# Head values multiplied by the output weights beforehand, four feature buffers, and the constant rows moved: a gated attention with mixture of experts on one core

## The reference

```python
# block 1: attention of 16 heads of 64, gated
qkv = x @ w_qkv.T; q, k, v = heads of qkv
gate = sigmoid of the scores of the 32 best tokens of a batch (by a small network on
       the mean of q over heads, layer-normalized), sigmoid(-1e9) for all others
dots = q k^T * 64**-0.5 * (gate_i * gate_j)
x = layernorm(x + (softmax(dots) v) @ w_out.T + b_out)
# block 2: causal attention of 16 heads of 8, then 8 experts of width 256, the best 2 of each token
x = x + mla(rmsnorm(x, g1)); x = x + moe(rmsnorm(x, g2), gate_w, w1, w2)
x = layernorm(...)
```

## Time and profile before

| | us |
|---|---|
| profiled execution, its own time | 694.79 |
| its span, first to last instruction | 692.7 |
| PE busy | 646.5 (93%) |
| DVE busy | 485.0 (70%) |
| ACT busy | 418.9 (60%) |
| POOL busy | 250.3 (36%) |
| mean PE clock granted, share of 2.4 GHz | 0.977 |

### The profile page before, as it was taken

One profiled execution on the slowest core, in us unless ns is written; L12 is line 12 of the kernel. 1 busy time (PEld: TensorE's weight loads), 2 busy tenths in 40 slices (PEclk: granted clock), 3 DMA queues, 4 the chain that ended last, 5 costly groups with the idle time before them and its releaser, 6 DMA issues.

```text
span 692.7 us, 14079 instructions
## 1 busy us (share of the span) xinstructions
PE 646.5 (93%) x5409; PEld 434.2 (63%) x5424; DVE 485.0 (70%) x1045; ACT 418.9 (60%) x764; POOL 250.3 (36%) x319
## 2 busy tenths in 40 slices
PE   7888798889899999999999999999999999999885
PEld 3476554455556667666766676766666667756774
DVE  2745556765687868876887787778777867754765
ACT  3452445666677666766675768575867676673431
POOL 8133101321333343344333533353334443443432
PEclk9999888999999999999999999999999999999998
DMA  8500000000000000000000000000000000000000
GB/s 317 183 18 16 1 1 1 1 2 1 1 1 1 1 1 2 17 1 1 1 18 1 1 2 16 2 1 2 17 1 2 1 16 1 1 16 1 1 16 16
DMA packets 10068, 12.15 MB, mean 18 GB/s; under 512 B 1609, under 2 KB 8210, under 8 KB 9746
## 3 DMA queue, kind: packets, MB, share of 16 engines
q1 hardware_dynamic: 9250, 11.25, 4.9%
q10 hardware_dynamic: 752, 0.01, 0.1%
HBM read 9.16 MB, written 2.10 MB: 16 GB/s over the span
## 4 chain that ended last, share of the span: by engine, by line
PE 70%; DVE 8%; ACT 5%; issue 3%; POOL 1%; POOLq 0%; ACTq 0%; DVEq 0%
PE turn L990 15%; PE turn L983 11%; PE psV L1043 11%; PE psW L1031 9%; PE psS L1016 6%; PE turn L945 5%; PE turn L935 3%; DVE negmax L1232 3%; PE psS L1005 2%; ACT prob L1151 2%; PE turn L953 2%; PE turn L964 1%; DVE late L1292 1%; ACT X L1062 1%; PE turn L884 1%
## 5 line engine op out<-in xcount | busy, mean ns | idle before, releaser
L1151 ACT ACTIVATE prob<-psW 128x1024 f32<-128x1024 f32 (+1 forms) x192 | 182.9, 953 | 108.1 <-PE psW L1031 107.8
L1232 DVE TENSOR_REDUCE negmax<-psS 128x2 f32<-128x1024 f32 (+2 forms) x249 | 198.9, 819 | 31.3 <-PE psS L1016 30.8
L853 POOL TENSOR_SCALAR_AFFINE_SELECT prob<-prob 128x512 f32<-128x512 f32 x128 | 79.8, 635 | 251.6 <-ACT prob L1151 251.6
L1292 DVE SCALAR_TENSOR_TENSOR late<-late,turn 128x512 f32<-128x512 f32 x128 | 87.5, 684 | 66.9 <-ACT late L1121 66.7
L990 PE MATMUL turn<-wexp,late 128*128 128x128 f32 x1024 | 129.3, 280 | 1.8 <-DVE late L1292 1.3
L990 PEld LDWEIGHTS turn<-wexp,late 128*128 128x128 f32 x1024 | 120.6, 193 | 10.1 <-issue 6.0
L1121 ACT ACTIVATE late<-turn 128x512 f32<-128x512 f32 x128 | 76.4, 597 | 63.0 <-PE turn L983 60.0
L861 POOL TENSOR_TENSOR late<-late 128x512 f32<-128x512 f32 x62 | 79.3, 1279 | 72.2 <-DVE late L1311 72.2
L1031 PE MATMUL psW<-qT,kT 26*128 26x256 f32 (+2 forms) x512 | 92.9, 399 | 8.7 <-ACT prob L1151 8.0
L1005 PE MATMUL psS<-kT,qT 24*128 24x256 f32 (+1 forms) x498 | 90.8, 401 | 1.0 <-DVE negmax L1232 0.9
L1031 PEld LDWEIGHTS psW<-qT,kT 26*128 26x128 f32 x512 | 43.1, 183 | 76.7 <-issue 52.6
(11 more groups left out here) (265 smaller groups left out, 894.9 us busy)
## 6 DMA issues: line engine op xcount, KB each, us to landing
prob<-in_xT SPq DMA_DIRECT2D x4, 512.0 KB, 6.4
X<-in_x SPq DMA_DIRECT2D x1, 2048.0 KB, 16.5
out<-late SPq DMA_DIRECT2D x8, 256.0 KB, 2.2
prob<-in_wqkvT SPq DMA_DIRECT2D x1, 1024.0 KB
late<-in_w SPq DMA_DIRECT2D x1, 1024.0 KB, 9.8
prob<-in_wqkvT SPq DMA_DIRECT2D x2, 256.0 KB, 3.7
late<-in_woutT SPq DMA_DIRECT2D x1, 512.0 KB
base_all<-base_rows SPq DMA_DIRECT2D x2, 256.0 KB, 3.2
```

The lines of the kernel that those rows point to most:

```text
L853: pool.affine_select(out=blk, in_=blk, compare_op=ALU.is_ge, fill=0.0, base=0, pattern=[[0, 4], [1, P]], channel_multiplier=-1).then_inc(s ...
L1151: A(into, src, ACT.Exp).then_inc(s["exp_ready"], 1)
L1232: last = V.tensor_reduce(negmax[:, u % 2, c, 2 * p:2 * p + 2], scores_in(b, n)[:, :, HALF * i:HALF * i + P * (c + 1)], AX, ALU.max, negate ...
L1292: V.scalar_tensor_tensor(out=hid[:, e % 2, k, :], in0=tanh[:, n % 2, :], scalar=1.0, in1=bank("hidden", b, n)[:, :], op0=ALU.add, op1=ALU. ...
```

## The change

In stage 1: (a) four feature buffers instead of two, and PE runs two features ahead; ACT takes the square root straight from PSUM with the epsilon as its bias, without DVE's pass. (b) Slot numbers start at 1, so that one DVE pass goes. (c) After the product of value and output weights over all heads, PE makes it for each head apart (`WVO`), and ACT copies it; the chosen tokens are multiplied with `WVO` instead of the value weights (four matmuls of 512 columns), and the heads' weights with that, all 16 added up in one bank; DVE gives the weights out in three parts. The outputs of the heads, their copies and the second product go. (d) The order around the gather: query and key matmuls wait only for the copied tokens; the base row comes after them; slot matmuls earlier; scores in two parts. (e) DVE adds the base rows of batches 0 and 1 in stage 1; POOL adds the other six in stage 2 (`rows`). `base_all` lies in the room of `oT`. In stage 2: (f) for batch 0 ACT takes a square root of variance terms for `xr`, in place of POOL's power; chunk by chunk signals; the first transposed half is handed over early; tables are loaded ahead by small activations. (g) Many places are changed, four of six `half parts` come between the first scores, and there are 32 fillers instead of 27.

```diff
-            A(Fc[:, t % 2, 0:HALF], ...) ; wait for v_done, g_ps at t - 1
+            A(Fc[:, t % 4, :], ...) ; wait for v_done, g_ps at t - 3
-                if t >= 1 and t + 1 < B:
-                    features(t + 1)
+                if t + 2 < B:
+                    features(t + 2)
-                V_.tensor_scalar(var[:, at], var_in[h][:, 0:HALF], LN_EPS, None, ALU.add).then_inc(g_used, 1)
+            for k in range(H):
+                i, rows = head_at(k) // 2, slice(DH * (k // NI), DH * (k // NI) + DH)
+                last = mm(bank[(0, 2, 3, 4)[k // 4]][:, D * (k % 4):D * (k % 4) + D], WvT[rows, i, :], WOUT[rows, i, :],
+                          start=True, stop=True, tile_position=(DH * (k // NI), 0))
...
-            unread(8)
+            for n in range(NH):
+                last = mm(bank[6 + n][:, :], selh[:, n, :], slot[:, :], start=True, stop=True)
...
+            for part, heads in enumerate(WEIGHTED):
+                pe.wait_ge(bdT_ready, part + 1)
+                pe.wait_ge(v_sb, heads.stop // 4)
+                for k in range(heads.start, heads.stop):
+                    last = mm(bank[1][:, 0:D], BDT[:, k, :], VW0[:, k, :], start=(k == 0), stop=(k == H - 1))
             last.then_inc(dl_ps, 1)
...
-            pool.wait_ge(bdT_ready, 1)
-            for b in BY_POOL:
-                ...
+            dve.wait_ge(base_in[0], 16)
+            for b in range(ROWS_EARLY):
+                V_.tensor_tensor(X[:, ts, :], X[:, ts, :], base_all[:, b, :]..., ALU.add)
...
-GATE_AT, SUM_AT, ADD_AT = 1.0, 1.21, 1.32
+GATE_AT, SUM_AT, ADD_AT = 1.0, 1.01, 3.42
-UNITS = {"usual": (13, 1.0, 3), 6: (13, 1.0, 3), 7: (13, 1.0, 4)}
+UNITS = {"usual": (13, 1.0, 3), 6: (13, 1.0, 3), 7: (14.5, 1.0, 4)}
-SELECT_AT = (2.0, 4.8, 5.2, 5.21)
-VALUE_AT = (4.0, 6.5, 6.5, 7.5)
+SELECT_AT = (2.3, 3.5, 4.2, 4.21)
+VALUE_AT = (4.0, 6.5, 7.5, 7.5)
-EARLY = {0: -40.35, 1: -37.2}
-NORMALIZE_EARLY = {0: -26.0, 1: -24.4}
-NORMAL_FROM = {2: 1.7, 3: 13.7, 4: 25.7, 5: 46.7, 6: 67.7, 7: 97.7}
+EARLY = {0: -41.35, 1: -25.1}
+NORMALIZE_EARLY = {0: -8.2, 1: -9.9}
+NORMAL_FROM = {2: -2.3, 3: 13.7, 4: 22.7, 5: 40.7, 6: 67.7, 7: 97.7}
-    ("half parts", 4): -39.85, ("half parts", 5): -39.75,
+    ("half parts", 2): -10.2, ("half parts", 3): -8.2, ("half parts", 4): -6.2, ("half parts", 5): -4.2,
-    UNREAD_AT: 27 places, from -11.2
+    UNREAD_AT: 32 places: -40.12, -40.11, -32.9, -30.0, -25.0, -24.5, -9.2, -7.2, -5.2, -1.2, -0.2, 0.8, 1.8, 2.8, ..., 187.3
+ROWS_FROM, ROWS_PITCH = -11.5, 1.5
...
+                if what == "rows":
+                    pool.wait_ge(keep["base_in"][b // HB], 16)
+                    pool.tensor_tensor(xb, xb, keep["base_all"][:, b, :]..., ALU.add).then_inc(s["rows_ready"], 1)
+                elif what == "first root" and b == 0:
+                    act.wait_ge(s["both_var"], 1)
+                    A(both[:, :], ve1[:, 0, 1, :], ACT.Sqrt).then_inc(s["both_root"], 1)
```

More of the change, by code:

```diff
@@ L172, in _ @@
                              ).then_inc(base_in[n], 16)
-            for n in range(NH):
-                sp.wait_ge(base_in[n], 16)
+            sp.wait_ge(base_in[0], 16)
         @block.gpsimd
@@ L308, in _ @@
             pe.wait_ge(masks, 2)
[L309 removed]
+            pe.wait_ge(std_ready, 1)
             unread(IN_GATE)
@@ L384, in _ @@
             base_rows(1)
-            pe.wait_ge(bdT_ready, 1)
-            pe.wait_ge(v_sb, 2)
-            for k in range(H):
-                h = head_at(k)
-                i = h // 2
-                rows = slice(DH * (h % 2), DH * (h % 2) + DH)
-                last = mm(bank[(6, 4)[i // 4]][rows, P * (i % 4):P * (i % 4) + P], V0[:, DH * h:DH * h + DH],
-                          BDT[:, k, :], start=True, stop=True)
-            last.then_inc(o_ps, 1)
-            pe.wait_ge(o_sb, 2)
-            for i in range(NI):
-                last = mm(bank[6][:, 0:D], OT[:, i, :], WOUT[:, i, :], start=(i == 0), stop=(i == NI - 1))
+            values(2)
+            values(3)
+            for part, heads in enumerate(WEIGHTED):
[3 more added lines that the diff above has]
+                    last = mm(bank[1][:, 0:D], BDT[:, k, :], VW0[:, k, :], start=(k == 0), stop=(k == H - 1))
             last.then_inc(dl_ps, 1)
@@ L442, in _ @@
             A(gv[:, :], scores[:, :], ACT.Sigmoid).then_inc(sig, 1)
+            for k in range(4):
+                act.wait_ge(wvo_ps, k + 2)
+                A(WVO[:, 4 * k:4 * k + 4, :], bank[(0, 2, 3, 4)[k]][:, :].rearrange("p (k d) -> p k d", d=D),
+                  ACT.Copy).then_inc(wvo_sb, 1)
             wqkv, wgate, wexp2, w1all = keep["wqkv"], keep["wgate"], keep["wexp2"], keep["w1raw"]
@@ L1081, in _ @@
                       ACT.Copy).then_inc(is_free("half outputs", 0, n), 1)
+                elif what == "first root" and b == 0:
+                    act.wait_ge(s["both_var"], 1)
+                    A(both[:, :], ve1[:, 0, 1, :], ACT.Sqrt).then_inc(s["both_root"], 1)
+                elif what == "nextT" and b == 0:
+                    A(xrT[:, 0:HALF], src[:, 0:HALF], ACT.Copy).then_inc(s["xrT_first"], 1)
+                    A(xrT[:, HALF:T], src[:, HALF:T], ACT.Copy).then_inc(is_free(what, b, n), 1)
                 elif what == "nextT":
@@ L1189, in _ @@
                 elif what == "offset":
+                    if b == 0:
+                        dve.wait_ge(s["both_root"], 1)
+                        own(V.reciprocal(both[:, :], both[:, :]))
+                        for c in range(C):
+                            V.tensor_scalar(xr[:, c, :], X[:, c, :], mv1[:, 0, c, 0:1], both[:, c:c + 1], ALU.subtract,
+                                            ALU.mult).then_inc(s["xr_first"], 1)
                     dve.wait_ge(s["rs1_ready"], b + 1)
```

279 lines of the change are left out of this document (152 added, 127 removed).

## The result

The changed kernel takes 689.55 us (median of 7 runs, 685.92 to 691.00) against 694.79 for the kernel before, measured beside it (7 runs). The ratio is 0.990, with a 95% interval of 0.9862 to 0.9938. All ratios and counts of runs in this document leave out those that lie over 1.5% above the fastest of their kernel (one of e2_add_early, two of e10_slots_and_fillers), while the medians are of all runs. Faster was right; the size was not: 678.5 was forecast, and 689.55 lies above the range of 672 to 686. The profiled execution took 689.55 us, with a span of 687.1.

A forecast was written before the change was run, and what follows sets the result against it. PE was taken to bound the full batches, and a chain through several engines everything before the first attention weights. Gains 8.1 + 5.6 + 1.5 + 1.5 - 0.4 = 16.3 took 694.8 to 678.5 us; range 672 to 686.

The forecast's parts named there:

- Feature buffers and bias row: Stage 1, 0 to 25 us: last variance 3 us earlier, mostly hidden by the bias-row wait; gain 0.3, bounds 0 to 2.9.
- Rival A: Stage 1: the bias row lands early, so PE doesn't wait for it; 2.6 us more gain, 675.9 us, chance 0.12.
- Rank and gather: Stage 1, ranking to scores: gains of 0.45, 1.35 and 0.65 us; second gather at 47.6 instead of 50.36.
- The product made beforehand: Stage 1: value-output products hidden; PE takes 12.0 us from second gather through heads; stage 2 at 60.2, whole stage gaining 8.1.
- Head of stage 2: Stage 2 start to first attention weights: 32.3 us instead of 37.9; gain 5.6, bounds 3.0 to 8.3.
- Rival B: Head of stage 2: it gives back all it gains; 684.1 us, chance 0.15.
- rival C: Stage 2: POOL's six row additions hold up every VectorE pass beside them, 8.8 us; 687.3 us, chance 0.06.
- First batch: First batch's attention: three added fillers fill idle time or lift the clock; -1.5 us, bounds +1.3 and -4.
- Tail: Last batch's end: first product 1 us later, following sequence closed up; -1.5 us, bounds +1 and -3.
- Rival D: Expert steps: later POOL additions free banks late and stall PE, 19 us over 64 steps; 697.7 us, chance 0.06.
- Rival E: Stage 1: heads wait for the fourth value copy instead of following the softmax parts; under 1 us, no separate chance.

The follow-up runs named there:

- e2_add_early: The changed kernel with POOL's additions of the experts' outputs and the residuals put back at their earlier places; 685.56 us, ratio 0.9855.
- e10_slots_and_fillers: The changed kernel with the eight fillers put back ahead of the four slot matmuls, which stay ahead of the gather; 687.31 us, ratio 0.985.
- e7_two_buffers: e3_slots_late with two feature buffers instead of four and the products of one step issued ahead; 684.89 us, ratio 0.9867.
- e1_bout_first: The changed kernel with the bias row loaded ahead of x instead of behind it; 688.16 us, ratio 0.9888.
- e3_slots_late: The changed kernel with the slot matmuls moved back behind the values and eight full fillers in their place; 683.34 us, ratio 0.9832.
- e11_slots_late_bare: The changed kernel with the four slot matmuls moved behind the values, but without the eight fillers; 689.96 us, ratio 0.9937.
- e14_fewer_fillers: The changed kernel without the three fillers that the change adds in the first batch's attention; 688.85 us, ratio 0.9901.
- e4_old_places: The changed kernel with all step places of stage 2 as before the change, stage 1 and each step's code as changed; 695.30 us, ratio 0.999.
- e5_select_early: e3_slots_late with the two places of e2_add_early, and POOL's first select of each group at 2.0 instead of 2.3; 680.62 us, ratio 0.98.
- e12_after_again: The changed kernel itself measured once more, with no difference; 690.47 us, ratio 0.9932.
- e9_all: e5_select_early with the bias row loaded ahead of x; 676.23 us, ratio 0.9739.

## Why the prediction was right or wrong

**Feature buffers and bias row: right, the exact time by luck.** The transposes at 20.34 (near 20.3 forecast) and the scores at 23.95 (near 24) answer to the first two signs that it named. The last variance came at 17.50, not near 16.6, since ScalarE's steps are 1.1 us apart and not 0.9; the wait for the bias row hides that. In the other profiles with the bias row behind x the transposes start between 20.3 and 22.2, so the 0.3 us of gain is smaller than what one execution differs from another. e7_two_buffers shows that the buffers bring nothing there that can be measured, and e1_bout_first that the wait was for the bias row. Rival A, worth 2.6 us, falls; that load ahead of x gives 2.2.

**Rank and gather: the step that failed.** "Four slot matmuls move into the place of eight fillers; I cost them at nothing, as they are about as long, though they put few rows into the array, which may bring the low clock on earlier." The danger was named and priced at zero, with a bound of 1.7 us for one more stretch at half clock anywhere in the stage. It came: the gather takes 2.6 us more and the key and query matmuls 0.9 more than the durations before, together 3.5 of the 3.6 that stage 2 starts late. e3_slots_late gets the chain back to its forecast, and e11_slots_late_bare shows that taking the fillers away is enough to lose it. So what was priced wrong is the loss of the fillers; the few rows of the slot matmuls, which the prediction named as the danger, are not shown to matter.

**The product made beforehand: right.** From the second gather on the forecast was 12.0 us to the end of the heads; it is 51.49 to 63.15, 11.7. The wvo products and their copies stay hidden under VectorE's ranking, as costed.

**Head of stage 2: right, 1.3 us too good.** Queries were forecast at +11.2 and came at +11.5; first weights at +32.3 came at +33.6. The prediction names additions of 2.2 and 1.6 us between the first scores and the first weights, but lets the stretch grow from 16.5 to 19.3 only; with both in full it is 20.3, and 20.2 was measured. That is 0.9 of the 1.3. Rival B, that the head gives back all, falls: 4.2 of the 5.6 us stay. Here the clock of the records is 1.00 from 48.1 to 98. In the kernel before it had two low stretches, 10.2 us together, so a part of that gain may be clock, which the prediction didn't count as such; how much isn't shown.

**POOL's row additions (rival C): falls.** They run in two groups of three, 1.27 us each (the first is the row at 82.01 above), between 82 and 90, and the VectorE passes beside them, which read one operand from PSUM, keep their length (0.29 and 0.28 us for the sums on qs and ks, the same at 87.80 beside POOL and at 91.85 without it). The port cost sits elsewhere, in the full batches, where the shift meets an expert's addition: 0.4 us a batch. The prediction gave the full batches no change, and named a change of over 0.5 as the sign that it is wrong.

**First batch: the second step that failed, wrong in sign.** The term was -1.5, with bounds of +1.3 and -4; +4.1 was measured. Three added fillers were to lift the clock. Instead there are 20.4 us at 1.2 GHz in two stretches (from 99.3 and from 130.0, 10.2 each), where before there was one of 6.8. e14_fewer_fillers shows that the fillers aren't it. The second stretch shows at its full 10 to 14 us in four of the nine profiles with a long gather, and in none of the six with the short one. Among the runs of the six kernels with fillers alone, 30 in all, none has a mean clock of 0.975 or less; of 40 runs of the changed kernel and its variants with the slot matmuls ahead of the gather (without e4_old_places) 23 do. So the exchange of fillers for slot matmuls moves the first batch, 40 us and more behind it. How it does so, and which half of it, is not shown. e11_slots_late_bare loses the clock in stage 1 for 13.7 us and has a first batch of 61.4 us, and only one of its seven runs stands so low. The 23 are also unevenly spread: one of five in e2_add_early, which differs only in places of stage 2, and none of four in e10_slots_and_fillers. This stays open.

**Tail: right, but by two errors.** Behind the first batch -1.5 for the end and +0.4 for a filler were forecast, -1.0 was measured. From the last attention weights on, the end is 2.9 us shorter, and the batches ahead of it took 1.9 back. The wait of the earlier trace rows is still there (between 620 and 690 us):

```profile
PE turn L1017 <- DVE late L1345: 1.8, 1, 1.8
```

So rank and combine ahead of the first gates didn't shorten it; what did shorten the end wasn't tried by itself. Rival D, PE stalling on banks kept by late additions, falls: between 200 and 624 us PE waits 4.0 us for the shift and 1.4 for exponentials of ScalarE. Rival E, that the heads wait for the last value copy, can't be told: they start at 59.42, with no idle time of PE ahead of them.

**The sum.** 3.6 + 1.3 + 5.6 + 0.1 = 10.6 of the 10.7 us between the forecast span and the measured one. Stage 1 and the first batch are 9.2 of it. With the fillers ahead of the gather 6.2 come back in the profile, 1.7 by the start of stage 2 and 4.5 in the first batch; another 2.0 are spent on the slot matmuls in their new place. The ratios say the same (0.983 for e3_slots_late in place of 0.990). POOL's order gives 0.4 us in each full batch (e5_select_early, 0.980, which is within the noise of 0.983).

## What to carry to other kernels

Work that only keeps PE fed is not free to replace: when fillers go, price the next 128-row matmuls at both clock levels (here a gather of 3.76 or 6.35 to 7.09 us), and put the difference into the range. Here it came in stage 1 and then once more in the first batch. Where a pass of VectorE that PE waits for runs beside POOL, look which POOL instruction is under way at that moment, and put the shortest one there. One execution of a kernel can differ from the next by its clock alone, so read a step of 1 us from several profiles. A wait that the profile hides behind busy work is worth removing only once the stretch behind it holds its clock.

## What the runs showed of the hardware

- PE can be busy without a gap and still fall to 1.2 GHz. In the changed kernel it is busy from 34.50 on, but for 0.1 us, with small transposes and then 1.96 us of 8-row matmuls, and falls at 37.8, 0.8 us into the gather. In the profiled run of e10_slots_and_fillers, a long one, it fell at 40.0 behind 1.90 us of full 128-row matmuls and 1.98 us of 8-row ones, with a gather of 6.46 us in place of 3.76.
- One order of instructions gives several clock histories. The six runs of e10 lie between 681.68 us (mean clock 0.991) and 693.02 (0.970); those of e3_slots_late between 682.41 and 684.90.
- A VectorE pass of 0.19 us with two SBUF inputs takes 0.55 us beside a select of POOL and 1.21 beside an addition, and ends with it to within 0.05 us (e5_select_early and the changed kernel). Sums that read one operand from PSUM took 0.28 to 0.29 us with and without an addition of POOL beside them.
- A load of 0.5 KB that is issued behind 2 MB by the same engine held PE until 20.34 in the changed kernel, and until 22.2 in another execution of it (e12_after_again). Issued ahead of them it freed the transposes by 18.16 (e1_bout_first) and 18.34 (e9_all).
